# Weighted values and their sums in one pass of 64x32 products, sums moved by transfers in SBUF

## The reference

```python
Q = query @ Wq + bq;  K = key @ Wk + bk;  V = value @ Wv + bv     # 32 query heads, 8 key/value heads, 16 wide
scores = einsum('bhgqd,bhkd->bhgqk', Q, K) * scale                # h: 8 key/value heads, g: 4 queries each
w = softmax(scores, axis=-1)
y = einsum('bhgqk,bhkd->bhgqd', w, V)
return y.reshape(B, S, EMBED) @ Wo + bo
```

## Time and profile before

| | |
|---|---|
| median of 3 runs | 690.85 us |
| the profiled execution | 692.62 us |
| its span, first to last instruction | 690.8 us |
| TensorE busy | 660.0 us (96%) |
| VectorE busy | 510.7 us (74%) |
| ScalarE busy | 432.8 us (63%) |
| GpSimd busy | 378.0 us (55%) |
| mean granted clock of TensorE | 0.986 of full |

### The profile page before, as it was taken

The page is one execution under the profiler, slowest core; times in us unless marked ns, Lnnn a source line. Parts: engine busy times, 40 slices in busy tenths (PEclk is TensorE's granted clock), DMA queues, the critical chain, the costliest instruction groups (busy, mean ns, idle before and its releaser), DMA issues.

```text
span 690.8 us, 12651 instructions
## 1 busy us (share of the span) xinstructions
PE 660.0 (96%) x3962; PEld 486.5 (70%) x3962; DVE 510.7 (74%) x1140; ACT 432.8 (63%) x794; POOL 378.0 (55%) x465
## 2 busy tenths in 40 slices
PE   8789999999989998999999999999999999999986
PEld 4446666666656576788787887787878878787775
DVE  4789899999967678677677776776777767774444
ACT  4668888888746775675746747558466574664221
POOL 2447999888866515345445354553545544534451
PEclk8799999999999999999999999999999999999999
DMA  8233534353234431112212222123121220211000
GB/s 268 75 129 102 154 105 152 95 186 116 65 106 108 128 113 50 47 50 63 72 31 61 60 61 61 34 57 87 35 61 47 61 75 30 61 28 50 17 16 30
DMA packets 32695, 54.37 MB, mean 79 GB/s; under 512 B 5360, under 2 KB 7152, under 8 KB 32656
## 3 DMA queue, kind: packets, MB, share of 16 engines
q1 hardware_dynamic: 32656, 53.90, 26.2%
HBM read 36.84 MB, written 8.39 MB: 65 GB/s over the span
## 4 chain that ended last, share of the span: by engine, by line
PE 78%; DVE 13%; issue 3%; ACT 2%; POOL 2%; DMA 0%; DVEq 0%; POOLq 0%; SPq 0%; ACTq 0%
PE wide L1294 7%; PE ps_b L1294 7%; PE wide L1296 6%; PE wide L1295 6%; PE ps_b L1296 6%; PE ps_b L1295 6%; PE ps_a L1339 4%; PE ps_b L1489 4%; PE wide L1407 4%; PE bank L1417 4%; PE ps_b L1349 3%; DVE gmax L1117 2%; PE ps_a L1294 2%; PE ps_a L1296 2%; PE ps_a L1295 2%
## 5 line engine op out<-in xcount | busy, mean ns | idle before, releaser
L779 POOL TENSOR_TENSOR va<-mv,small 128x1 f32<-128x1 f32 x80 | 15.4, 193 | 154.9 <-DVE mv L1273 79.2
L744 ACT ACTIVATE stage<-wide 128x512 f32<-128x512 f32 x30 | 16.3, 595 | 83.6 <-PE bank L1590 83.5
L867 POOL TENSOR_TENSOR y_l<-y,y_h 128x512 fp32r<-128x512 f32 x16 | 21.9, 1372 | 72.4 <-ACT y_h L652 72.4
L1141 DVE RECIPROCAL y<-ps_b 128x256 f32<-128x256 f32 x32 | 55.9, 1748 | 0.4 <-PE ps_b L1489 0.4
L675 ACT ACTIVATE probs<-wide 128x1024 f32<-128x1024 f32 x32 | 32.8, 1026 | 35.8 <-PE wide L1543 35.8
L1294 PE MATMUL wide<-up_h,t_h 128*128 128x512 f32 x128 | 52.4, 409 | 1.5 <-DVE t_l L1225 1.5
L1296 PE MATMUL wide<-up_h,t_l 128*128 128x512 f32 x128 | 50.6, 396 | 0.0
L1295 PE MATMUL wide<-up_l,t_h 128*128 128x512 f32 x128 | 50.3, 393 | 0.0
L1294 PE MATMUL ps_b<-down_h,ht_h 128*128 128x512 f32 x120 | 49.5, 413 | 0.4 <-DVE ht_l L1213 0.4
L781 POOL TENSOR_TENSOR rs<-va,small 128x1 f32<-128x1 f32 x80 | 44.6, 558 | 6.3
L1296 PE MATMUL ps_b<-down_h,ht_l 128*128 128x512 f32 x120 | 47.1, 392 | 0.0
(11 more groups left out here) (245 smaller groups left out, 2166.0 us busy)
## 6 DMA issues: line engine op xcount, KB each, us to landing
q_stack<-qt_h SPq DMA_DIRECT2D x128, 64.0 KB, 2.0
ctx_t<-in_ctx SPq DMA_DIRECT2D x16, 256.0 KB, 2.7
x_res<-in_x SPq DMA_DIRECT2D x16, 256.0 KB, 2.9
x_in<-x_rows SPq DMA_DIRECT2D x16, 256.0 KB, 2.7
ctx_t<-in_ctx_turned SPq DMA_DIRECT2D x16, 256.0 KB, 2.9
x_res<-x_rows SPq DMA_DIRECT2D x16, 256.0 KB, 3.0
out<-stage SPq DMA_DIRECT2D x15, 256.0 KB, 3.0
x_in<-in_x SPq DMA_DIRECT2D x8, 256.0 KB, 2.9
```

Source lines behind the costliest of these rows:

```text
L1141: dve.reciprocal(y[:, :, b, :], part[:, 1]).then_inc(S["den_s"], 1)
```

## The change

The two products (values, ones) become one. `vbd` is filled with ones, not zeros, outside the values' blocks. For each sequence b, pair p and head h of the pair a product takes only the 64 rows of that head: its 32 output rows are the weighted values of head h in h's 16 rows, and the sums of head h in the 16 rows beside them. It goes to bank 2+h, so there are 16 products a tile of 64 rows by 32 columns of the array, against 16 of 128 by 32.

Then numerators and sums are brought together. ScalarE copies both banks to SBUF (`sums[0]`, `sums[1]`) and makes `y` from bank 2, scaled by a column `place[0]` that is one in the rows of head 0. VectorE adds `sums[1]` times `place[1]` to it. SyncE moves each head's sums (16 rows by 512 columns, eight transfers a tile) from the rows beside to the head's own rows, into `den`, and VectorE takes one reciprocal over `den` and multiplies `y` by it. The new waits: SyncE for `sums_s`, VectorE for `sums_s` and for `den_in` (all eight transfers landed). `attend_ready` puts TensorE's waits for `attend` before `turned_hidden(i, 0)`.

```diff
-            dve.memset(vbd[:], 0.0).then_inc(S["vbd_zero"], 1)
+            dve.memset(vbd[:], 1.0).then_inc(S["vbd_zero"], 1)
@@ SyncE @@
+            def denominators(t):
+
+                if live(t):
+                    sp.wait_ge(S["sums_s"], 2 * t + 1)
+                    wait(sp, S["wo_ps"], t)
+                    for h in range(2):
+                        for p in range(PAIRS):
+                            at, beside = STACK * p + HD * h, STACK * p + HD * (1 - h)
+                            sp.dma_start(den[at:at + HD], sums[h][beside:beside + HD]).then_inc(S["den_in"], 16)
...
             def body2(i):
                 load2(i + 4)
                 stacked(i + 3)
+                denominators(i + 2)
                 residual(i + 2)
@@ ScalarE @@
+            def attended_out(t):
+
+                if live(t):
+                    act.wait_ge(S["pv_ps"], 2 * t + 2)
+                    act.wait_ge(S["qy_ps"], capped(1, t + 2))
+                    for h in range(2):
+                        last = act.activation(sums[h][:].rearrange("p g b q -> p b g q"),
+                                              bank[2 + h].rearrange("p (b g q) -> p b g q", b=2, g=GROUPS), ACT.Copy)
+                    last.then_inc(S["sums_s"], 1)
+                    wait(act, S["wo_ps"], t)
+                    act.activation(y[:].rearrange("p g b q -> p b g q"),
+                                   bank[2].rearrange("p (b g q) -> p b g q", b=2, g=GROUPS), ACT.Copy, scale=place[0]
+                                   ).then_inc(S["sums_s"], 1)
...
                 if live(t) and not final(t):
                     hidden_high(t, 0)
+                attended_out(i + 2)
@@ VectorE @@
+            def numerators(t):
+
+                if live(t):
+                    dve.wait_ge(S["sums_s"], 2 * t + 2)
+                    dve.scalar_tensor_tensor(y[:], sums[1][:], place[1], y[:], ALU.mult, ALU.add).then_inc(S["den_s"], 1)
+
             def attended(t):
                 if live(t):
-                    wait(dve, S["wo_ps"], t)
-                    for b in range(2):
-                        part = bank[2 + b].rearrange("p (n g q) -> p n g q", n=2, g=GROUPS)
-                        dve.wait_ge(S["pv_ps"], 2 * t + b + 1)
-                        dve.reciprocal(y[:, :, b, :], part[:, 1]).then_inc(S["den_s"], 1)
-                        dve.wait_ge(S["den_s"], 2 * t + b + 1)
-                        dve.tensor_tensor(y[:, :, b, :], part[:, 0], y[:, :, b, :], ALU.mult).then_inc(S["y_s"], 1)
+                    dve.wait_ge(S["den_in"], DEN_MOVES * (t + 1))
+                    dve.reciprocal(den[:], den[:]).then_inc(S["den_s"], 1)
+                    dve.wait_ge(S["den_s"], 2 * t + 2)
+                    dve.tensor_tensor(y[:], y[:], den[:], ALU.mult).then_inc(S["y_s"], 1)
@@ TensorE @@
-            def attend(t):
+            def attend_ready(t):
                 if live(t):
                     pe.wait_ge(S["vbd_s"], t + 1)
                     wait(pe, S["kv_s"], capped(1, t + 2))
                     wait(pe, S["z_s"], t - 2)
+                    pe.wait_ge(S["probs_s"], 2 * t + 2)
+
+            def attend(t):
+
+                if live(t):
                     for b in range(2):
-                        pe.wait_ge(S["probs_s"], 2 * t + b + 1)
-                        for n in range(2):
-                            for p in range(PAIRS):
-                                lhs = ones_bd if n else vbd[:, b, p].rearrange("k h d -> k (h d)")
-                                last = pe.matmul(bank[2 + b][32 * p:32 * (p + 1), 256 * n:256 * (n + 1)], lhs,
-                                                 probs[:, b, p, :], start=True, stop=True)
+                        for p in range(PAIRS):
+                            for h in range(2):
+                                k = slice(SEQ * h, SEQ * (h + 1))
+                                last = pe.matmul(bank[2 + h][STACK * p:STACK * (p + 1), HALF * b:HALF * (b + 1)],
+                                                 vbd[k, b, p].rearrange("k h d -> k (h d)"), probs[k, b, p, :],
+                                                 start=True, stop=True)
                         last.then_inc(S["pv_ps"], 1)
...
                 turned_queries(i + 3)
+                attend_ready(i + 2)
                 t = i
                 if live(t) and not final(t):
                     turned_hidden(t, 0)
```

More of the change, by code:

```diff
@@ L36 @@
 IDENT0 = FIRST
-HEAD0, PAIR0, ONES0, HALF0 = IDENT0 + P, IDENT0 + 136, IDENT0 + 138, IDENT0 + 170
+HEAD0, PAIR0, PLACE0, HALF0 = IDENT0 + P, IDENT0 + 136, IDENT0 + 138, IDENT0 + 140
 EPS0, MINUS0, SEL0 = HALF0 + 1, HALF0 + 2, HALF0 + 3
@@ L93, in constants @@
     small[:, HEAD0:HEAD0 + PART] = np.tile(np.repeat(np.eye(PART), HD, axis=0), (2, 1))
-    small[:, ONES0:ONES0 + 2 * HD] = np.kron(np.eye(2), np.ones((SEQ, HD)))
+    small[:, PLACE0:PLACE0 + 2] = np.tile(np.repeat(np.eye(2), HD, axis=0), (PAIRS, 1))
     for p in range(PAIRS):
@@ L135, in build @@
         head_of_pair = small[:, PAIR0 - FIRST:PAIR0 - FIRST + 2]
-        ones_bd = small[:, ONES0 - FIRST:ONES0 - FIRST + 2 * HD]
+        place = [small[:, PLACE0 - FIRST + h:PLACE0 - FIRST + h + 1] for h in range(2)]
         half, eps, minus = (small[:, c - FIRST:c - FIRST + 1] for c in (HALF0, EPS0, MINUS0))
@@ L157, in build @@
         x_in, ctx_t = sb("x_in", [P, D]), sb("ctx_t", [P, D])
+        with ExitStack() as tmp:
+            sums = [sb(f"sums{h}", [P, GROUPS, 2, SEQ], stack=tmp) for h in range(2)]
         x_h, x_l = sb("x_h", [P, D], F32R), sb("x_l", [P, D], F32R)
@@ L233, in build @@
         y_flat = y[:].rearrange("p g b q -> p (g b q)")
+        with ExitStack() as tmp:
+            den = sb("den", [P, GROUPS, 2, SEQ], stack=tmp)
         y_h = sb("y_h", [P, D], F32R)
@@ L246, in build @@
             sel_in sel_s qs_s ql_s ql0_s kp_s qkt_ps kt_hi kt_lo qt_hi qt_lo qt_bs kbd_s vbd_s g_ps gmax_s gmt_ps ngm_s s_ps probs_s
-            pv_ps den_s y_s y_hi y_lo wo_ps x2b_s x3_s x3b_s x3c_s
+            pv_ps sums_s den_in den_s y_s y_hi y_lo wo_ps x2b_s x3_s x3b_s x3c_s
             t4_ps t4_hi t4_lo u_ps relu_s h_s top_s rw_s rt_out_ps routed_s
@@ L252, in build @@
             stage_hi stage_lo
-            dft_hi dft_lo c1_hi c1_lo nm1_s nb1_s nm2_s nb2_s x_loaded x_odd_loaded ctx_loaded res_loaded bn1_s mv1_s va1_s rs1_s xn1_s
-            q_ps qf_s k_ps prod_s v_ps vf_s vsw_s corr_ps tops_s shift_s exp_s rep_s sum_s inv_s sub_s wgt_s
+            dft_hi c1_hi c1_lo nm1_s nb1_s nm2_s nb2_s x_loaded x_odd_loaded ctx_loaded res_loaded bn1_s mv1_s va1_s rs1_s xn1_s
+            q_ps qf_s k_ps prod_s v_ps vsw_s corr_ps tops_s shift_s exp_s rep_s sum_s inv_s sub_s wgt_s
             wt_ps wt_s wf_ps prod2_s o_ps x1_s bn2_s mv2_s va2_s rs2_s xn2_s
@@ L285, in build @@
         MOVES = 16 * 2 * PAIRS
+        DEN_MOVES = 16 * 2 * PAIRS
         EARLY = NT - 2
@@ L485, in turn_two @@
                 stacked(1)
+                denominators(0)
                 store(LAST)
@@ L619, in body @@
                     wait(act, S["prod2_s"], t - 1)
-                    act.activation(v[:, 0].rearrange("p b n -> p (b n)"), ps_b[:], ACT.Copy).then_inc(S["vf_s"], 1)
+                    act.activation(v[:, 0].rearrange("p b n -> p (b n)"), ps_b[:], ACT.Copy)
                     act.wait_ge(S["shift_s"], t + 1)
@@ L646, in keys_stacked @@
                     stack(k_pairs, kt_l, (1,)).then_inc(S["kp_s"], 1)
+            def attended_out(t):
[10 more added lines that the diff above has]
+                                   ).then_inc(S["sums_s"], 1)
             def y_high(t):
                 if live(t):
-                    act.wait_ge(S["y_s"], 2 * t + 2)
+                    act.wait_ge(S["y_s"], t + 1)
                     wait(act, S["wo_ps"], t)
@@ L701, in turn_two @@
                 merged_high(0)
+                attended_out(0)
                 context_high(2)
                 keys_stacked(1)
+                merged_high(1)
                 y_high(0)
-                merged_high(1)
                 merged_high(2)
@@ L1014, in _ @@
             dve.wait_ge(S["dft_hi"], 1)
-            dve.tensor_tensor(dft_l[:], dft[:, K0:W0], dft_h[:].bitcast(F32), ALU.subtract).then_inc(S["dft_lo"], 1)
+            dve.tensor_tensor(dft_l[:], dft[:, K0:W0], dft_h[:].bitcast(F32), ALU.subtract)
             first_context(0)
@@ L1192, in turn_two @@
                 queries_low(1)
-                attended(0)
+                numerators(0)
                 merged_low(0)
                 maxima(1, 0)
+                attended(0)
                 context_low(2)
@@ L1232, in body2 @@
                     hidden_low(t, 0)
+                numerators(i + 2)
                 attended(i + 2)
@@ L1567, in turn_two @@
                 merge(0)
+                attend_ready(0)
                 attend(0)
@@ L1633, in body2 @@
                 if live(t) and not final(t):
-                    wait(pe, S["y_s"], capped(2, t + 3))
```

(1 more changed line is left out.)

## The result

| | before | after |
|---|---|---|
| median of the runs | 691.03 us (4 runs, 690.18 to 691.28) | 831.26 us (4 runs, 827.3 to 835.94) |
| ratio, with its 95% interval | | 1.2035 (1.1966 to 1.2103) |
| span of the profiled execution | 690.8 us | 827.7 us |
| mean granted clock | 0.986 | 0.91 |

What follows compares the result with a forecast made beforehand. TensorE was taken as the bound, in flight 28.02 of 28.10 us a turn. Thirteen turns x 8.5 = 110.5, with tile 0 (9), tile 1 (10.5) and tile 15 (4), made 134, so 690.85 became 825 us; range 772 to 848.

Steps and rivals of the forecast that it cites:

- TensorE's saving: Attention products on TensorE: half the array rows each, 0.86 us less a tile, bounds 0 and 0.93.
- SyncE: SyncE's queue: eight issues for `den` behind those for `q_stack`, 0.62 us each, decide when the transfers go out.
- The bound of 0.36: Other end for one issue's time on SyncE: 0.36 us, from the residual's transfer (128 rows from memory).
- 2.0 us to land: Landing of each 32 KB transfer into `den`: 2.0 us, taken from the 64 KB row.
- VectorE: VectorE after the transfers land: reciprocal of 512 columns in one piece 3.34 us, then the product with `y` 0.68.
- The stand: TensorE before the output product: stands still 7.2 us for `y_l`; the product begins 6.3 us later than now.
- Behind it: VectorE's queue, next norm, `x3` and routed product after the stall: all late, a turn 7.3 us longer at full clock.
- The clock: TensorE's clock after each stall: falls to 1.2 GHz, lengthening a turn to 7.9 to 9.7 us more, taken 8.5.
- its sign: What would show the clock's fall: granted clock 0.5 right after the output product's start.
- The sum: Whole kernel: 13 turns x 8.5, plus tiles 0, 1 and 15, together 134 us more.
- rival 1: Transfers into `den` hidden, only TensorE's saving counts: 16 x 0.86 = 13.8 us less, 677 us; chance 3%.
- the waits of `attend_ready`: TensorE's waits brought forward before the hidden layer's transposes: cost at most 0.2 us.

Runs made afterwards that it cites:

- e4: Changed kernel with the attention's sixteen products run twice, same result: 832.03 us, ratio 1.203 to the kernel before.
- e3: Changed kernel with 26 matmuls of 128x512 into a free bank in each tile, before TensorE's wait for `y_l`: 812.65 us, ratio 1.1744 to the kernel before.
- e11: e1 with VectorE's sum of the two best experts written as a reduction of one operand: 695.58 us, ratio 1.007 to the kernel before.
- e1: Changed kernel without the transfers into `den`; the reciprocal reads ScalarE's copy as it lies (wrong rows): 696.06 us, ratio 1.0044 to the kernel before.
- e7: Changed kernel with one `stream_shuffle` swapping the halves of the sums instead of the transfers, right rows: 692.25 us, ratio 0.999 to the kernel before.
- e12: e7 with tiles 0 and 1 by the way of the kernel before, ones filled in ahead of tile 2: 687.08 us, ratio 0.9935 to the kernel before.
- e13: e12 with the order of turn two as in the kernel before, on VectorE and ScalarE: 683.57 us, ratio 0.9894 to the kernel before.
- e5: Kernel before with only the 64x32 products and the waits brought forward; no copies or transfers, output not the weighted mean: 686.04 us, ratio 0.9912.

## Why the prediction was right

Step by step, in the turn that starts at 627.21 (after) and at 474.78 (before).

- **TensorE's saving**: 0.86 taken, 0.83 measured. That its size doesn't enter was shown by e4.
- **SyncE**: the eight issues for `den` right behind `q_stack`'s, 0.62 each and the last 10.3 us after the attention's start; measured 4.93/8 = 0.62 and 10.0. The bound of 0.36 from the residual's row was the wrong kind of transfer, as argued. The page has 2.0 us to land ("den<-sums SPq DMA_DIRECT2D x128, 32.0 KB, 2.0"), as taken.
- **VectorE**: 3.34 for the reciprocal, 3.35 measured; 0.68 for the product, 0.69.
- **The stand**: the output product was to start 18.6 us after the attention's and starts after 18.26; 0.27 of the difference is that the issues for `den` begin 5.72 after the attention's start, not 5.99. 7.2 us of stand, 6.8 in this turn and 7.0 on average.
- **Behind it** the forecast was right in sum and off in its parts. At full clock a turn was to be 7.3 longer; e3 measures 35.02 - 28.06 = 7.0. VectorE's top-2 sum was counted at the 0.82 of the earlier trace rows and took 0.16, and `c_l` took 1.20 for 0.68. Neither time belongs to the operation: they are the hold by GpSimd that e11 shows. Before, the sum ended with `x_res` (483.80 to 485.08 on GpSimd, the sum until 485.10); after, `c_l` starts at 644.76, while `y_l` runs until 645.41. The two errors nearly cancel, and that is luck. The clock was to cost between 0.6 and 2.4, taken 1.2; measured 1.4. The 1.2 was a choice inside that range that no row fixed, so part of the closeness is luck too. The prediction had the low clock behind the stand. It falls inside it, so 3.6 of the 6.8 us at the low level are spent standing (641.9 to 645.5); its sign, 0.50 right after the output product's start, holds.
- **The sum**: 8.5 a turn against 8.56; tile 0 9 against 10.4; tile 1 10.5 against 11.7; tile 15 4 against 5.8. In all 134 against 136.8, with the 2.3 less ahead of tile 0 taken off. The other 3.4 of the 6 us between 825 and 831.26 are that after's profiled execution (829.46) lies 1.8 below the median of its runs and before's (692.62) 1.6 above.

**Where it was wrong**: rival 1, "the transfers are hidden and the kernel is faster", was priced at 677, by all of the 16 x 0.86. e1 is that case, and it took 696. The step that fails is that "only TensorE's saving counts". With the transfers gone the path to `y_l` still has a reciprocal in one piece behind copies by ScalarE, so it is longer than before. The two opening turns are 5.7 us longer. e1 was not taken apart there, but e7's 6.1 were: 3.4 came back with the old way for tiles 0 and 1 (e12), and 2.1 with the old order in turn two (e13), so not all of it is the path. In the steady turns GpSimd's `y_l` moves onto VectorE's sum, which reads two SBUF operands, so that of the 0.66 that e5 has there only 0.16 is left (over the 13 turns 2.3 us of 6.9). The prediction also put the waits of `attend_ready` at up to 0.2 us and then left them out of rival 1. e5's 0.66 against 0.83 is that term: from the last product of the turned queries to the attention's start it takes 0.83 us (471.29 to 472.12), and before it took 0.64 (474.14 to 474.78). The hold in the steady turn is shown by e1 against e5; that e7 escapes it because `c_l` slips in between is read from its rows only.

## What to carry to other kernels

Count the issues, not the bytes: a chain that waits for eight small transfers from one queue waits for eight issue times, and what stands ahead of them in that queue counts as much. If data must cross partitions within 32 rows, look for an operation of the engine that uses them anyway: the shuffle took 0.73 us where eight transfers took 6.3. A saving on the bounding engine is worth nothing in front of a wait, and little where the next engine's pace lies right beside it: look which two-operand work of VectorE stands beside GpSimd's before pricing it.
